# A GpSimd power for layer 1's queries, moved behind the second pair's normalisation

## The reference

```python
x = x + _L0_xattn_ref(_layernorm(x), ctx_1024, ...)   # 16 heads of 64
x = x + _L0_ffn_ref(_layernorm(x), ...)               # 8-bit rows, ternary weights, conv of 3, silu
x = x + _L1_xattn_ref(_layernorm(x), ctx_1024, ...)   # 16 heads of 16
x = x + _L1_ffn_ref(_layernorm(x), ...)               # 8-bit with one scale over all batches
```

```python
def rms_norm(x, w):
    var = jnp.mean(x * x, axis=-1, keepdims=True)
    return x * jax.lax.rsqrt(var + EPS) * w

q = rms_norm(q, q_norm_w)          # over the 16 numbers of each of 16 heads
q = apply_rope(q, q_cos, q_sin)
attn = softmax(einsum('bhtd,bhsd->bhts', q, k) * scale)
```

## Time and profile before

| what | value |
|---|---|
| median of 3 runs | 2382.2 us (2381.74 to 2383.67) |
| profiled execution, its own time | 2380.98 us |
| its span in the profile | 2379.2 us |
| mean granted clock of TensorE | 0.989 of full speed |
| PE busy | 2294.8 us, 96% of the span |
| DVE busy | 1663.5 us, 70% |
| POOL busy | 1628.8 us, 68% |
| ACT busy | 1510.5 us, 63% |
| share of PE in the chain of work that ended last | 92% |

### The profile page before, as it was taken

How to read it: one execution, slowest core, us unless ns; L and a number is a source line. 1 busy time by engine, 2 the same in 40 slices (tenths; PEclk the granted TensorE clock), 3 DMA queues, 4 the chain that set the end, 5 groups by cost and what they waited for, 6 DMA issues and landing times.

```text
span 2379.2 us, 61055 instructions
## 1 busy us (share of the span) xinstructions
PE 2294.8 (96%) x20320; PEld 1774.9 (75%) x20320; DVE 1663.5 (70%) x4061; ACT 1510.5 (63%) x4306; POOL 1628.8 (68%) x1830
## 2 busy tenths in 40 slices
PE   6999999999999999999999999999999999999578
PEld 5777777777787777777777777787777777777336
DVE  6766666776767667766666776767667666666785
ACT  4666666666666666666666666666666666666356
POOL 3676776676768767676776676767767676776507
PEclk9999999999999999999999999999999999999689
DMA  4000000000000000000000000000000000001202
GB/s 146 10 11 10 10 8 10 2 10 10 10 10 8 10 2 10 10 10 10 10 8 9 3 10 10 10 10 8 10 2 10 10 10 10 10 2 38 54 10 63
DMA packets 31197, 37.04 MB, mean 16 GB/s; under 512 B 3284, under 2 KB 29636, under 8 KB 31172
## 3 DMA queue, kind: packets, MB, share of 16 engines
q1 hardware_dynamic: 31172, 36.71, 5.3%
HBM read 29.36 MB, written 7.34 MB: 15 GB/s over the span
## 4 chain that ended last, share of the span: by engine, by line
PE 92%; DVE 3%; POOL 2%; issue 2%; ACT 1%; DMA 0%; POOLq 0%; SPq 0%; ACTq 0%; DVEq 0%
PE ps L349 25%; PE ps L410 17%; PE pt L434 11%; PE pa L446 7%; PE pt L424 5%; PE ps L393 5%; PE pa L486 4%; PE pa L461 4%; PE pa L349 2%; PE pt L349 2%; PE pa L584 1%; PE pt L609 1%; PE ps L474 1%; DVE th L1412 1%; PE pa L624 1%
## 5 line engine op out<-in xcount | busy, mean ns | idle before, releaser
L1048 DVE TENSOR_REDUCE nmx<-ps 112x2 f32<-112x750 f32 x512 | 480.1, 938 | 197.0 <-PE ps L410 190.9
L1508 POOL TENSOR_TENSOR prob<-prob,rinv 112x375 f32<-112x375 f32 x512 | 404.9, 812 | 197.6 <-DVE rinv L1056 197.6
L1508 POOL TENSOR_TENSOR f1w_room<-f1w_room,rinv 112x375 f32<-112x375 f32 x512 | 405.4, 817 | 64.3 <-DVE rinv L1056 64.3
L768 ACT ACTIVATE room<-ps 128x375 f32<-128x375 f32 (+2 forms) x480 | 227.8, 488 | 303.9 <-PE ps L349 303.9
L768 ACT ACTIVATE probT<-pt 125x336 f32<-125x336 f32 (+1 forms) x512 | 242.6, 474 | 195.8 <-PE pt L424 142.1
L808 ACT ACTIVATE prob<-ps,nmx 112x375 f32<-112x375 f32 x512 | 289.8, 580 | 65.7 <-DVE nmx L1048 65.7
L808 ACT ACTIVATE f1w_room<-ps,nmx 112x375 f32<-112x375 f32 x512 | 291.2, 587 | 2.4 <-DVE nmx L1048 2.3
L1533 POOL TENSOR_TENSOR krs<-krs,nhalf 125x48 f32<-125x48 f32 x32 | 256.9, 8030 | 0.0
L410 PE MATMUL ps<-kT,q 64*112 64x375 f32 x1024 | 234.6, 517 | 1.0 <-ACT prob L808 1.0
L410 PE MATMUL ps<-room,q 64*112 64x375 f32 x1024 | 230.7, 515 | 3.0 <-ACT prob L808 1.9
L1039 DVE COPY probT<-pt 125x336 f32<-125x336 f32 x322 | 162.7, 505 | 96.2 <-PE pt L434 96.2
(11 more groups left out here) (270 smaller groups left out, 5326.0 us busy)
## 6 DMA issues: line engine op xcount, KB each, us to landing
craw<-in_ctx SPq DMA_DIRECT2D x32, 375.0 KB, 3.1
xin<-in_x SPq DMA_DIRECT2D x32, 112.0 KB, 2.0
x_rows<-x SPq DMA_DIRECT2D x32, 112.0 KB, 1.9
out<-probT SPq DMA_DIRECT2D x16, 224.0 KB, 2.3
room<-x_rows SPq DMA_DIRECT2D x1, 2576.0 KB, 12.8
w<-in_f1w SPq DMA_DIRECT2D x2, 1024.0 KB, 6.7
stage<-in_wk SPq DMA_DIRECT2D x1, 1024.0 KB, 7.3
stage<-in_wv SPq DMA_DIRECT2D x1, 1024.0 KB, 9.8
```

Source lines behind the costliest of these rows:

```text
L768: return act.activation(dst, src, ACT.Copy)
L1048: top = dve.tensor_reduce(nmx[:, g:g + 2], ps[0:T, 2 * (i % 2):2 * (i % 2) + 2, 0:S], AX_X, ALU.max, negate=True)
L1508: pool.tensor_tensor(prob(i, n), prob(i, n), rinv[:, g:g + 1].to_broadcast([T, S]), ALU.mult).then_inc(s["normed"], 1)
```

## The change

On POOL, in the 31 turns of the loop, `query_root(1)` goes behind the two multiplications of pair 1; it stood between `query_root(0)` and these. On DVE, `query_scale(b, 1)` goes from the end of step 1 to the end of step 2, on PE `query_turn(b, 1)` from step 3 to step 4, and on ACT `query_copies(b)` from step 3 to step 4. The last batch keeps its order. No instruction is added or removed, and SP's list is the same.

```diff
@@ tensor, attention
-                    if part == MIDDLE and i == 3:
+                    if part == MIDDLE and i == 4:
                         query_turn(b, 1)
@@ vector, attention
-                    if part == MIDDLE and i == 1:
+                    if part == MIDDLE and i == 2:
                         query_scale(b, 1)
@@ gpsimd, rest
                 query_root(0)
-                query_root(1)
-                attention(part, b, 0 if last_batch else 1, PAIRS if last_batch else G)
+                if last_batch:
+                    query_root(1)
+                    attention(part, b, 0, PAIRS)
+                else:
+                    attention(part, b, 1, 2)
+                    query_root(1)
+                    attention(part, b, 2, G)
```

## The result

The changed kernel takes 2397.6 us at the median of 5 runs (2395.8 to 2404.41), the kernel before 2381.74 us in the same comparison (2380.6 to 2383.67). The ratio is 1.0074, with a 95% interval from 1.0055 to 1.0092: slower, clear of the 0.2% bound. The forecast was 2394.9 us in a range of 2385 to 2402. The profiled execution of the changed kernel took 2397.6 us itself, with a span of 2395.8 us. Three of the five runs (2395.8 to 2397.6 us) have a mean granted clock of 0.986 to 0.987 and two (2403.42 and 2404.41 us) one of 0.983; what decides that was not tried.

A forecast was written before the change was run, and what follows sets the result against it. PE was taken to bound the loop; 0.39 us standstill plus 0.02 us for ACT made 0.41 us a turn, x 31 = 12.7 us, 2393.7 profiled, 2394.9 us forecast with the 1.2 us to the median, range 2385 to 2402.

The forecast's parts named there:

- The bound and the place: PE sets the loop's pace, with 0.27 us idle a turn; a move is worth its effect on that idle time.
- POOL's sum: POOL idles 0.79 us before pair 1; pair 1 ready 0.85 us sooner, pair 2's second head some 0.75 us later, at 1135.22.
- Turn(2)'s standstill: On PE in turn(2), the wait for pair 2's second head from POOL: 0.39 us of new standstill a turn.
- "same" rival: Lag from POOL nearer 0.05 than 0.21 us, or unseen slack; standstill below 0.15 us a turn, 2382 to 2387; chance 0.16.
- The transpose's move: PE's transpose of the queries takes 0.19 us out of step 3 into step 4; 0 over the turn.
- Turn(1) and scores(5): Turn(1) gains up to 0.25 us on PE, but scores(5) waits for pair 3's exponentials: worth 0.
- The port: DVE's moved scale meets POOL's pair 2 at the shared port: 0 if POOL is first, up to 0.28 us if DVE is.
- ACT's copies: Copies ahead of turned(4) and exps(7) in step 4; scores(9) covered by 0.1 us only; 0.02 us on the mean.

The follow-up runs named there:

- run nine: Kernel before with one swap on DVE in step 1, turned(0) ahead of row_sum(2): 2380.07 us in one run, beside a median of 2380.87 for before.
- run two: Kernel before with only PE's transpose of the queries and ACT's copies moved to step 4: 2389.13 us, ratio 1.0031.
- Runs four to six: Kernel before plus one one-column PE product: 128 rows in step 4, 2387.2 us; 64 rows there, 2381.59 us; 128 rows in step 3, 2381.66 us.
- run three: Kernel before with only ACT's four masked copies moved to step 4, transpose left in step 3: 2381.54 us, ratio 0.9998.

## Why the prediction was right, and where its terms were off

**The bound and the place** held. PE sets the turn, it has no idle time that takes a new standstill up, and the clock in the loop stayed at 1.00. What did not hold is that an edit is worth what it does to PE's idle time. With the same 18481 instructions PE's busy time in the loop rose by 2066.86 - 2051.21 = 15.65 us, more than the 14.91 us of the loop: the profile books both losses, the wait in turn(2) and the transpose's dear place, as busy time.

**POOL's sum** held to some hundredths. Pair 1 was said to start 0.07 us behind its rinv and POOL to idle 0.79 us; it idled 0.75. Pair 2's second head was said to be ready at 1135.22, which in the changed trace's time is 1144.71; it was ready at 1144.68.

**Turn(2)'s standstill, the main term, was too large: 0.39 us predicted, some 0.25 measured** (its weights at 1144.73; unmoved they would be at about 1144.48). The step that failed is the lag from POOL's end to PE. I took 0.21 us from turn(1), whose weights came that long behind pair 1. But turn(1) was held by DVE's copy of pair 0, as run nine shows. The true lag stands in the changed kernel: ready at 1144.68, weights at 1144.73, 0.05 us. The "same" rival named that lag, and it came true; but the standstill did not shrink below 0.15 us, as that rival had it. With 0.25 us alone the forecast would have been 2390 (0.25 x 31 = 7.8 us over 2382.2), still slower.

**The transpose's move, put at 0, cost 0.22 to 0.24 us**: 0.32 in the new place less 0.10 in the old on the timeline, 0.24 by the loop of run two. This term was the second step that failed. I read 0.19 us from start to start in the old place and carried it to the new one as if an instruction had one price. Runs four to six show that its neighbours make it.

**Turn(1) and scores(5)**: the worth of 0 came out, for another reason. Turn(1) didn't start sooner at all, because DVE's copy held it and not POOL. The reason given, that scores(5) would swallow the gain, failed for the 0.06 us that run nine tried: turn(2) came 0.06 us sooner. How much more would have passed is open; scores(5) starts there 0.05 us behind the last read of pair 3's exponentials (1134.80, 1134.85), so the margin is small.

**The port**: L1073 took 0.90 us instead of 0.28, it waited for POOL's multiplication and not the other way round (pair 2 took its usual 1.58 us), and row_max(5) came at 1144.75 instead of 1144.21. PE felt nothing of it, as the working had it: its cover was ACT's and PE's other work. Beside a power no such wait shows: in the kernel before, the first half's L1073 took 0.29 us at 1129.84, while POOL was in its second power until 1131.31.

**ACT's copies**, put at 0.02 us with a thin cover of 0.1 us, cost nothing (run three). In the changed kernel exps(7)'s last read ended at 1152.24 and scores(9) began at 1152.59, so the cover was 0.35 us. (The of scores(7) and scores(9) show three of four products; each one's first is 0.12 us ahead of them.)

The sum was 0.41 us a turn and the loop has 0.50: 0.39 + 0.02 predicted, about 0.25 + 0.24 measured. Two errors of opposite sign, 0.14 and 0.24 us, hid each other. The direction and the place of the wait were foreseen; that the time came within 2.7 us of the forecast is luck. Of the 2.7 us between forecast and median, 0.09 x 31 = 2.8 us are the loop's; the 1.9 us at the start and the 0.7 us at the end are not the change's.

## What to carry to other kernels

Moving a slow instruction behind a quicker one helps only if the quicker one can start: find what releases it, and count the idle time that opens as delay for everything behind. Don't bound what a move costs by the idle time of the busiest engine: here both losses are booked as busy time. An instruction on TensorE has no price of its own; read what two neighbours cost from start to start with it and without it, above all where row-tiled work passes into row-tiled work. Where two producers end within 0.1 us of each other, don't take a lag from the one that the profile names.

## What the runs showed of the hardware that I had not expected

A product of one column over 128 rows costs 0.16 us between transposes of 64 or 48 rows and products of 64 rows, and nothing with 64 rows in the same place or with 128 rows among neighbours over all rows.

A standstill of 1.42 us, with 0.24 us shortly behind it, once in each turn of otherwise dense work went with a granted clock that fell in many turns (mean of 0.96 over the loop, 135 us with the delay itself). Two useless products in the gap kept it at 1.00 and gave 85 us back. The standstill of 0.25 us in the changed kernel did nothing of the kind.
